# Sixteen-head attention: queries and keys held as two float16 parts instead of three bfloat16 parts, scores in one matmul of 50 rows

## The reference

```python
Q, K, V = (proj(W_Q), proj(W_K), proj(W_V))          # 16 heads of 16
Q = _apply_rope(Q, cos, sin)
K = _apply_rope(K, cos, sin)
scores = jnp.einsum('bhsd,bhtd->bhst', Q, K) / jnp.sqrt(jnp.float32(D_K))
scores = jnp.where(causal[None, None], scores, -jnp.inf)
attn = jax.nn.softmax(scores, axis=-1)
out = jnp.einsum('bhst,bhtd->bhsd', attn, V)
```

## Time and profile before

| | us |
|---|---|
| median of 3 runs | 2640.6 (2639.23 to 2643.33) |
| span of the profiled execution | 2633.8 |
| PE busy | 2442.8 |
| DVE busy | 1990.4 |
| ACT busy | 1552.1 |
| POOL busy | 597.8 |

### The profile page before, as it was taken

How to read it: one execution, slowest core, us unless ns; L and a number is a source line. 1 busy time by engine, 2 the same in 40 slices (tenths; PEclk the granted TensorE clock), 3 DMA queues, 4 the chain that set the end, 5 groups by cost and what they waited for, 6 DMA issues and landing times.

```text
span 2633.8 us, 57555 instructions
## 1 busy us (share of the span) xinstructions
PE 2442.8 (93%) x21618; PEld 1121.3 (43%) x21618; DVE 1990.4 (76%) x4256; ACT 1552.1 (59%) x2785; POOL 597.8 (23%) x584
## 2 busy tenths in 40 slices
PE   6898799999999999999899999999999999999995
PEld 4544333434445353443444444353444533433344
DVE  4777888887858879687877787878686798788822
ACT  2335466665655656565555766656565566666761
POOL 5564210304133040311314112130313300000011
PEclk9999899999999999999999999999999999999997
DMA  2433220212213122130311313121131222111110
GB/s 54 115 83 93 85 82 20 73 49 62 69 34 87 55 82 57 50 90 21 86 49 49 101 50 90 26 74 55 41 83 34 72 62 61 39 48 40 30 43 26
DMA packets 225600, 159.33 MB, mean 60 GB/s; under 512 B 91824, under 2 KB 225072, under 8 KB 225328
## 3 DMA queue, kind: packets, MB, share of 16 engines
q1 hardware_dynamic: 224560, 154.75, 21.2%
q10 hardware_dynamic: 768, 0.92, 0.1%
HBM read 87.36 MB, written 67.63 MB: 59 GB/s over the span
## 4 chain that ended last, share of the span: by engine, by line
PE 65%; DVE 20%; ACT 5%; issue 4%; SPq 2%; POOL 2%; DMA 2%; DVEq 1%; POOLq 0%; ACTq 0%
PE psum L1777 14%; PE psum L1754 13%; DVE mx L1475 12%; PE psum L1725 7%; PE psum L1691 4%; ACT probs L1249 3%; PE psum L1655 2%; PE psum L1808 2%; PE psum L1565 2%; PE psum L1626 2%; PE psum L1828 2%; PE psum L1816 2%; PE psum L1797 2%; PE psum L1595 2%; PE psum L1712 2%
## 5 line engine op out<-in xcount | busy, mean ns | idle before, releaser
L1249 ACT ACTIVATE probs<-psum 128x512 f32<-128x512 f32 x2176 | 1142.5, 604 | 557.4 <-PE psum L1754 311.0
L1475 DVE TENSOR_REDUCE mx<-psum 128x1 f32<-128x512 f32 (+2 forms) x2304 | 1289.1, 620 | 239.7 <-PE psum L1725 183.7
L1754 PE MATMUL psum<-qst,kst 34*128 34x512 bf16 (+7 forms) x5120 | 659.5, 349 | 46.8 <-DVE mx L1475 15.7
L1777 PE MATMUL psum<-probs,vs 128*17 128x512 f32 (+3 forms) x5120 | 581.9, 536 | 0.7
L1725 PE MATMUL psum<-kst,qst 64*128 64x512 bf16 (+3 forms) x2560 | 427.5, 351 | 37.0 <-DVE mx L1475 16.2
L1754 PEld LDWEIGHTS psum<-qst,kst 64*128 64x128 bf16 (+1 forms) x5120 | 193.7, 94 | 393.5 <-ACT probs L1249 117.0
L1725 PEld LDWEIGHTS psum<-kst,qst 64*128 64x128 bf16 x2560 | 129.2, 93 | 348.4 <-ACT probs L1249 141.0
L1777 PEld LDWEIGHTS psum<-probs,vs 128*17 128x17 f32 x5120 | 93.0, 95 | 183.2 <-issue 153.3
L1043 POOL TENSOR_SCALAR vare<-mv 128x4 f32<-128x4 f32 x64 | 15.3, 239 | 562.4 <-DVE mv L1351 562.4
L1072 POOL TENSOR_TENSOR sums<-probs 128x512 f32<-128x512 f32 x12 | 15.3, 1272 | 529.4 <-ACT probs L1199 529.4
L1732 PE MATMUL psum<-maskq,identh 64*128 64x64 bf16 (+1 forms) x2048 | 126.9, 204 | 0.0
(11 more groups left out here) (160 smaller groups left out, 2839.7 us busy)
## 6 DMA issues: line engine op xcount, KB each, us to landing
qk_dram<-parts SPq DMA_DIRECT2D x224, 128.0 KB
qst<-qk_dram SPq DMA_DIRECT2D x384, 64.0 KB, 2.1
kst<-qk_dram SPq DMA_DIRECT2D x384, 64.0 KB, 2.0
v_dram<-vst SPq DMA_DIRECT2D x64, 136.0 KB, 3.9
vs<-v_dram SPq DMA_DIRECT2D x64, 136.0 KB, 2.1
xs<-x_in SPq DMA_DIRECT2D x16, 512.0 KB, 3.9
x_dram<-xs SPq DMA_DIRECT2D x16, 512.0 KB, 2.9
att_dram<-ast SPq DMA_DIRECT2D x64, 128.0 KB, 2.0
```

The costliest lines, as they stand in the source:

```text
L1249: act.activation(dst, src, ACT.Exp, scale=DK1 ** -0.5).then_inc(S["exp"], 1)
L1475: ins = dve.tensor_reduce(mx1[:, n % 2, 2 * g + odd, tile % TPC, c:c + 1], bank(src, at, at + cols), AX.X, ALU.max)
L1754: ins = pe.matmul(two[odd][:, at:at + cols], kst[rows, kslot, part, pair, keys], qst[rows, qslot, part, pair, CH - cols:CH], start=(part = ...
L1777: ins = pe.matmul(bank(7, off, CH, rows=VW, row=32 * h), vtile[:, h, :], probs[:, HG * (step_no(b, hg, k) % 2) + h, at:at + CH - off], sta ...
```

## The change

The projection weights for q and k are rescaled once at the start. Six small jobs (`wsquare`, `wsum`, `wtotal`, `wbase`, `wroot`, `wscale`) find a power of two from the ratio of the two norms, so that q and k have a like size, and multiply both by 4 (`LIFT`); the exponential divides by 16 again. `QK1` waits for `wscale`. q and k are then held in two float16 parts: `hi` as before, and `res` writes the remainder straight as the second part; `mid` and `lo` are gone. Three copies of 16 rows are stored, q as (hi, hi, rest) and k as (hi, rest, hi), so 48 rows hold the products. The negated maximum, divided by 32768 and split in two float16 rows, stands in rows 48 and 49 against 32768 in `kst`. So `scores` is one pair of 50-row matmuls per piece, and `max` uses 48 of the same rows. `load q` and `load k` are two DMAs each instead of six, `put` three instead of four. `nmax` has one small DVE instruction more. Besides, the exponential of layer 0 on the diagonal is taken in two instructions that leave out the unwritten part, and `V0` waits for the weights itself.

```diff
-PARTS = 3
-STORED = ((0, 1, 2, 0), (0, 1, 0, 2))
-PAIRED = ((0, 0), (0, 1))
+STORED = ((0, 0, 1), (0, 1, 0))
+PARTS = 2
+PROWS = len(STORED[0]) * DK1
+LIFT = 4.0
+UNIT1 = 32768.0
...
+        add("POOL", "wsquare", c, key(0), 2.7, ("root", (0, *c)), lat=6.0)
+        add("DVE", "wsum", c, key(0), 1.2, ("wsquare", c))
+        add("PE", "wtotal", c, key(0), 0.2, ("wsum", c), lat=0.1, claim="P", mode="F")
+        add("DVE", "wbase", c, key(0), 0.2, ("wtotal", c), free=("wtotal", c))
+        add("POOL", "wroot", c, key(0), 1.5, ("wbase", c))
+        add("DVE", "wscale", c, key(0), 2.0, ("wroot", c))
...
-        add("DVE", "res", (*c, bl), key(0.3), 0.61, ("hi", (*c, bl)), ("lo", old), free=("RT", (*c, bl)))
-        add("ACT", "mid", (*c, bl), key(0.3), 0.53, ("res", (*c, bl)))
-        add("POOL", "lo", (*c, bl), key(0.3), 1.12, ("mid", (*c, bl)))
-        add("SP", "put", (*c, bl), key(0.3), 0.6, ("lo", (*c, bl)), lat=5.0)
+        add("DVE", "res", (*c, bl), key(0.3), 0.61, ("hi", (*c, bl)), free=("RT", (*c, bl)))
+        add("SP", "put", (*c, bl), key(0.9), 0.5, ("res", (*c, bl)), lat=4.0)
...
-                add("PE", "scores", (b, hg, k, j), key + j, 0.43 * size + (0.09 * len(pieces) if diagonal else 0),
+                add("PE", "scores", (b, hg, k, j), key + j, 0.215 * size + (0.09 * len(pieces) if diagonal else 0),
...
-        kst = sb("kst", [P, KRING, 2, HG // 2, CH], BF16)
-        qst = sb("qst", [P, QRING, 2, HG // 2, CH], BF16)
+        kst = sb("kst", [P, KRING, HG // 2, CH], F16)
+        qst = sb("qst", [P, QRING, HG // 2, CH], F16)
...
-                        for part, row, first in [(0, 0, PAIRED[side][0]), (0, REST, PAIRED[side][1]), (1, 0, 2)]:
-                            row += HALF * odd
-                            sp.dma_start(into[row:row + REST, slot, part, :, :],
-                                         of[first:first + 2, :, :, :].rearrange("n d g t -> (n d) g t")
-                                         ).then_inc(loaded, 16)
+                        sp.dma_start(into[HALF * odd:HALF * odd + PROWS, slot, :, :],
+                                     of.rearrange("n d g t -> (n d) g t")).then_inc(loaded, 16)
...
-                        pool.memset(kst[:, pieces, 1, :, :], 1.0).then_inc(done, 1)
+                        pool.memset(kst[:, pieces, :, :], UNIT1).then_inc(done, 1)
...
+                elif kind == "wsquare":
+                    pool.memset(wones, 1.0).then_inc(S["ones"], 1)
+                    pool.memset(wnorm[:, 1, 0:1], -0.25).then_inc(S["ones"], 1)
+                    pool.memset(wnorm[:, 1, 1:2], 0.25).then_inc(S["ones"], 1)
+                    wt.wait_ge("weights q", 32)
+                    pool.tensor_tensor(wsquares, wqk1[:, :, :], wqk1[:, :, :], ALU.mult).then_inc(S["wsquare"], 1)
...
-                    act.activation(probs0[:, n % 2, :, 0:cols], two_banks("scores0", item)[:, :, 0:cols], ACT.Exp,
-                                   scale=DK0 ** -0.5).then_inc(S["exp0"], 1)
+                    if lo:
+                        act.activation(probs0[:, n % 2, 0, 0:cols], two[:, 0, 0:cols], ACT.Exp, scale=DK0 ** -0.5)
+                        ins = act.activation(probs0[:, n % 2, 1, lo:cols], two[:, 1, lo:cols], ACT.Exp, scale=DK0 ** -0.5)
+                    else:
+                        ins = act.activation(probs0[:, n % 2, :, 0:cols], two[:, :, 0:cols], ACT.Exp, scale=DK0 ** -0.5)
...
+                elif kind == "wscale":
+                    power = wnorm[:, 3, 0:1].bitcast(I32)
+                    link(dve.tensor_scalar(power, power, 0x7F800000, None, ALU.bitwise_and))
+                    link(dve.reciprocal(wnorm[:, 3, 1:2], wnorm[:, 3, 0:1]))
+                    for side in range(2):
+                        cols = wqk1[:, :, D * side:D * (side + 1)]
+                        ins = dve.tensor_scalar(cols, cols, wnorm[:, 3, side:side + 1], LIFT, ALU.mult, ALU.mult)
...
-                    link(dve.tensor_copy(nmaxb[:, :, 0, :, :], minus))
-                    dve.tensor_tensor(nmaxb[:, :, 1, :, :], minus, nmaxb[:, :, 0, :, :], ALU.subtract
-                                      ).then_inc(S["nmax"], 1)
+                    link(dve.tensor_scalar(nmaxb[:, :, 0, :, :], minus, 1.0 / UNIT1, None, ALU.mult))
+                    for odd in range(2):
+                        ins = dve.scalar_tensor_tensor(out=nmaxb[:, odd, 1, :, :], in0=minus[:, odd, :, :],
+                                                       scalar=1.0 / UNIT1, in1=nmaxb[:, odd, 0, :, :],
+                                                       op0=ALU.mult, op1=ALU.subtract)
...
-                            rows = slice(HALF * odd, HALF * (odd + 1))
+                            rows = slice(HALF * odd, HALF * odd + PROWS)
                             ins = pe.matmul(two[odd][:, at:at + cols],
-                                            qst[rows, qslot, 0, pair, P * (tile % TPC):P * (tile % TPC + 1)],
-                                            kst[rows, kslot, 0, pair, 0:cols], start=True, stop=c < q)
+                                            qst[rows, qslot, pair, P * (tile % TPC):P * (tile % TPC + 1)],
+                                            kst[rows, kslot, pair, 0:cols], start=True, stop=c < q)
...
-                        for part in range(2):
-                            for odd in range(2):
-                                rows = slice(HALF * odd, HALF * odd + (HALF if part == 0 else RROWS))
-                                ins = pe.matmul(two[odd][:, at:at + cols], kst[rows, kslot, part, pair, keys],
-                                                qst[rows, qslot, part, pair, CH - cols:CH],
-                                                start=(part == 0), stop=(part == 1 and not diagonal))
+                        for odd in range(2):
+                            rows = slice(HALF * odd, HALF * odd + PROWS + MAXROWS)
+                            ins = pe.matmul(two[odd][:, at:at + cols], kst[rows, kslot, pair, keys],
+                                            qst[rows, qslot, pair, CH - cols:CH], start=True, stop=not diagonal)
```

More of the change, by code:

```diff
@@ L426, in chunk_jobs @@
             ("rows0", c), ("qk0", (*c, 1)), lat=0.1, claim="D", mode="R")
-        add("ACT", "exp0", (*c, kp), key(0.6), 0.17 + 0.853 * size, ("scores0", (*c, kp)), ("values0", old), ("sum0", old),
+        add("ACT", "exp0", (*c, kp), key(0.6), 0.17 + 0.853 * size + (0.05 if diagonal else 0), ("scores0", (*c, kp)), ("values0", old), ("sum0", old),
             free=("scores0", (*c, kp)))
@@ L1687, in _ @@
                     b, q, t = item
-                    wt.wait_ge("weights q", 32)
+                    wt.job("wscale", (0, 0))
                     turned(wt, 2, b, q)
@@ L1734, in _ @@
                     ins.then_inc(S["max"], 1)
+                elif kind == "wtotal":
+                    wt.wait_ge("ones", 3)
+                    wt.job("wsum", item)
+                    pe.matmul(home(kind, item)[:, 0:2], wones, wnorm[:, 0, :], start=True, stop=True
+                              ).then_inc(S["wtotal"], 1)
                 elif kind == "turnmax":
```

79 lines of the change are left out of this document (44 added, 35 removed).

## The result

| | before | changed |
|---|---|---|
| median (range) | 2639.9 us (2638.5 to 2643.3) | 2563.6 us (2562.6 to 2574.4) |
| ratio, 95% interval | | 0.972 (0.970 to 0.974) |
| profiled execution's span | 2633.8 us | 2562.6 us |

The changed kernel is faster by 76 us in the medians, and by 71 us between the two profiled executions. The prediction had 190 us, 2450 us with a range of 2392 to 2520: the sign is right, the size is not, and the time lies outside the range.

What follows compares the result with a forecast made beforehand. PE was taken to set the pace, narrowly ahead of DVE; savings of 183 (middle), 4 (start) and 4 us (tail) took the span from 2633.8 to 2442.8, plus 6.8 around it: 2450 us, range 2392 to 2520.

Steps and rivals of the forecast that it cites:

- The score pass: Score matmuls on PE: halved to the max pass's shape, their busy time falls from 659.5 to 427.5 us, 232 less.
- third rival: PE matmuls: float16 runs slower than bfloat16; at 0.44 us a pair the time is 2880 us; chance 0.03.
- DVE keeps its work: DVE: the 2304 reductions, 1289.1 us, stay; the maximum's split adds 13 us; 1742 us of work in the middle.
- The middle: Span from 330 to 2508 us: saves 183 us, from PE's share falling as DVE's rises to about 88%.
- second rival: Middle: DVE sets the pace and holds 85% at most, saving 129 us there; time 2504 us; chance 0.17.
- fourth rival: PE's clock: a tenth of the middle's PE work at 1.2 GHz costs 186 us; time 2636 us; chance 0.03.
- The start: First 330 us: 6 us less PE work, 3 us lost to preparation, 1 us from dropped third-part steps; saves 4 us.
- The preparation: Start: the weights' norm and rescaling jobs on DVE, POOL and PE cost 0 to 6 us, taken as 3.
- The tail: Stage after 2508 us: 5.8 us of PE work go where PE is at 76%, saving 4 us.
- Edits at nothing: Fewer stores and loads, layer 0's split diagonal exponentials and V0 ahead of QK0: put at nothing, traffic a few us at most.
- What lies around the span: Time outside the profiled span: 6.8 us up to the median of 2640.6, taken to stay unchanged.
- first rival: Whole kernel: PE alone sets the time and DVE follows; time put at 2400 us; chance 0.16.

Runs made afterwards that it cites:

- e15: Kernel before, with the planner trying 48 instead of 8 random orders for each 40 us stretch: 2645.4 us, 1.003 of before.
- e7: Changed kernel with layer 1's DVE max reductions and ACT exponentials both on half their columns, same order, part of the calculation left out: 2393.4 us.
- e13: Changed kernel with layer 1's ACT exponentials on half their columns, DVE reductions whole, same order: 2548.0 us.
- e11: Changed kernel with six instead of seven PSUM banks for the score products of both passes, no work changed, order laid out anew: 2672.3 us.
- e6: Changed kernel with layer 1's max reductions reading half their columns and the planner told, so the order is laid out for it: 2427.2 us.
- e5: Changed kernel with layer 0's values (V0) put behind the projection of its queries and keys (QK0) again: 2572.9 us.
- e14: Changed kernel with the planner trying 48 instead of 8 random orders for each 40 us stretch: 2539.3 us, 0.963 of before.
- e3: Kernel before with only the 34-row score pass, the other part's products left out, bfloat16 and three stored parts kept, planner told: 2548.0 us.
- e12: Changed kernel with the layer norms' scaling, 256 instructions, moved from DVE to POOL, planner told 2.0 us a job: 2617.5 us.
- e1: Changed kernel with layer 1's max reductions on DVE reading half their columns, order unchanged: 2489.2 us, 0.943 of before.

## Why the prediction was wrong, point by point

- **The score pass, -232 us of PE work: right.** 659.5 became 434.7 us, 354 ns each; float16 costs what bfloat16 did (below), the third rival is out.
- **DVE keeps its work: right.** 1740 us in the middle against 1742, reductions of 621 ns. The split of the maximum came to 6 us more in all (30.6 against 24.6), not 13.
- **The middle, -183 us: wrong, it gave 68 (72 with the other cut).** This is the step that failed. I drew a line through pieces of the kernel before (PE's share against DVE's) and followed it to DVE at 88%. The line doesn't hold for the changed kernel: at DVE's 82.5% it says 95.1% for PE, and PE had 91.7%. A straight line through all whole 66 us pieces of the middle, and not eight chosen ones, passes 94.8% at that place before and 91.9% in the changed kernel; and in e15, the kernel before in another order, PE's share doesn't hang on DVE's at all (correlation 0.00, where it is -0.55 before). So it was a feature of one order of one kernel. It also made DVE the only partner, while e7 and e13 show that ACT counts too, and e11 that PE's pace depends on the banks that both of them hold. That a heavy piece borrows from its light neighbours, as my second rival said of its 89.8%, may add to it and wasn't tested. At 82.5% DVE is a little under even the 85% of the second rival, which gave 2504 us: the rival had a cause of the right kind in part, was too mild, and had 0.17.
- **PE's busy time, -156 where -232 was said.** The rest isn't work but slower work. At 1.2 GHz PE's clock stood for 99 us before, in which PE was busy for 71, and for 202 us in the changed kernel, with 169 busy (from the granted clock in both traces). If what runs there takes twice its time, as the sixteen value matmuls did (3.65 and 1.89 us), that is (169 - 71) / 2 = 49 us more. It is an estimate, and rather too high: the clock's records begin only at 29 us before and at 19 in the changed kernel. The other 20 to 30 are overlap: PE's groups, each taken by itself, add up to 535 us more than PE's busy time before, and to 506 more in the changed kernel, so 29 us less of them lie side by side. The fourth rival gave this 186 us and a chance of 0.03. It came true in part: the middle has 80 us at 1.2 GHz instead of 24. That this follows from the waits is likely (e6 has 110 us of idle time of PE between 330 and 2310 us, and 24 us at 1.2 GHz) but no run changes the clock alone. By the Trainium skill ("TensorE: Matmul & The Clock Gate", section "HAM oscillation — how this bites in real kernels"), such returns to half rate follow where PE stands idle between bursts; the traces agree as to direction, with a mean granted clock of 0.98 in the middle against 0.99 and idle time of PE there up from 102 to 175 us.
- **The start, -4 us: wrong sign, +12.** I costed `V0` ahead of `QK0` at nothing, as a shift of 2 us that others cover. e5 shows that it costs 7 of the 10 us by which layer 1 comes late: in the first microseconds nothing else is there to cover it, and it fell into a stretch at half clock. The preparation, taken as 3 us, may be the other 3; no run isolates it. Rows of the two starts, 0 to 66 and 66 to 132 us, first before:

```profile
0.00:66.00 66.00, 45.03 (x217) 27.67 (x218) 31.09 (x87) 17.04 (x21) 34.62 (x58) 0.93 0.22 54
66.00:132.00 66.00, 57.19 (x302) 35.99 (x302) 49.52 (x115) 25.03 (x36) 38.03 (x34) 0.94 0.43 116
```

and the changed kernel:

```profile
0.00:66.00 66.00, 45.22 (x195) 27.35 (x197) 29.62 (x81) 14.84 (x20) 30.24 (x56) 0.79 0.18 45
66.00:132.00 66.00, 50.60 (x215) 32.47 (x214) 40.85 (x103) 14.33 (x22) 30.74 (x31) 0.82 0.28 78
```

- PE was busy as long in the first piece, but got through 195 matmuls instead of 217. The clock is at 0.79, where it was at 0.93, but time without a record counts as full speed: e14 has 0.95 there, with records from 39 us only, though its value matmuls take the same 3.65 us.
- **The tail, -4 us: it gave 15.** Its PE time fell by 13 us, not 5.8, with 44 matmuls fewer than the halved score pass explains: 4 of the 15 us are the place of the cut (above), and the rest is also the order's; no run parts them.
- **Edits at nothing:** right for the traffic. HBM reads fell from 87.4 to 62.2 MB (pages of the two kernels), the chain's DMA share stayed at 2%, and e3, with all the old traffic, has a middle as short as the changed kernel's.
- **What lies around the span, 6.8 us: too much.** The changed kernel's profiled execution took 2564.5 us with a span of 2562.6, and the other runs have 1.7 to 2.2 us in the same way. The rest of the 6.8 is that the profiled execution of before was, by the same measure, some 5 us faster than its median, which is also why 76 us of the medians stand against 71 of the spans.
- **The first rival,** PE alone and 2400 us, needs DVE and ACT out of the way: e7 comes nearest to that, with 2393 us. That the numbers agree is in part luck, since PE is still idle for 8% of it and its own order was kept.

Open: how much of the missing 115 us in the middle is the banks' holding time itself, how much the clock (some 27 us by the estimate above: 76.7 us busy at 1.2 GHz in the middle, 23.4 before) and how much an order that could still be better. A six-fold search found 24 us; nothing here shows how far it goes. That the change is worth 106 us there rests on one draw of each. And with DVE light and the order laid out anew the score pass gives 151 us, not 232.

## What to carry to other kernels

When an engine at 95% gets 10% lighter, and a partner at 80% takes its results out of a few shared buffers, don't read the new balance off single stretches of the old kernel: how the two shares hang together there belonged to its order, and moved by 3 points with the change. Ask how long a buffer is held, by whom, and which part of that the change shortens; the quickest test is to take one buffer away, or to halve the partner's work and see what the change is worth then. Where a random search lays out the order, time each version with two draws before believing 20 us, and don't put an edit at zero in the first 100 us, where nothing is there to cover it.

## What the runs showed of the hardware

- Float16 matmuls of 48 and 50 rows run at the rate of bfloat16 ones of 64 and 34: the starts below are 0.22 us apart for a pair of 512 columns, as in the earlier trace rows.

```profile
1499.71 0.39 PE L1793 MATMUL psum<-qst,kst 50*128 50x512 f16 x2
1499.93 0.71 PE L1760 MATMUL psum<-kst,qst 48*128 48x512 f16 x4
```

- PE can be busy for 89% of a span and still have 200 us at 1.2 GHz: 202 of 2563 in the changed kernel, 161 in e14, 140 in e7, and 236 in e12, which has the longest waits for norms (the first 19 to 39 us of each have no record of the clock).
- One PSUM bank of seven was worth 109 us of 2564 (e11), more than the 76 us that the change gave.
- A 128x256 float32 scaling took 1226 ns on POOL (e12) and 460 ns on DVE (changed kernel).
- Halving the columns of a reduction from PSUM took its group's mean from 621 to 387 ns (e1). If the time goes straight with the columns, 387 - 234 = 153 ns of each don't depend on them (an estimate).
